# Attention with a mixture of experts on one core: other slots for the routing parts and the row sends

## The reference

```
xn = layernorm(x)
out = x + attention(xn) + experts(xn)

attention: 16 heads of width 8, causal;
  scores = q k^T / sqrt(8) - log1p(decay_h * log1p(distance))
  y = softmax(scores) v,  times w_proj

experts: 8 experts, 128 -> 512 -> 128
  probs = softmax(xn Wr^T); the two best experts of each token,
  their weights normalised to sum 1
  sum over the two of weight * (silu(xn W1_e^T) W2_e^T)
```

## Time and profile before

| | |
|---|---|
| median of three runs | 505.39 us |
| the profiled execution's own time | 506.12 us |
| its span, first to last instruction | 504.40 us |
| granted TensorE clock, mean | 0.997 |
| busy: PE, DVE, ACT, POOL | 478.1, 365.7, 336.6, 366.2 us |
| sends: 64, mean of one | 982 ns |
| POOL's subtractions: 388, mean of one | 493 ns |
| DVE's score instructions: 512, mean of one | 485 ns |

### The profile page before, as it was taken

One profiled execution on the slowest core, in us unless ns is written; L12 is line 12 of the kernel. 1 busy time (PEld: TensorE's weight loads), 2 busy tenths in 40 slices (PEclk: granted clock), 3 DMA queues, 4 the chain that ended last, 5 costly groups with the idle time before them and its releaser, 6 DMA issues.

```text
span 504.4 us, 13425 instructions
## 1 busy us (share of the span) xinstructions
PE 478.1 (95%) x4294; PEld 346.7 (69%) x4294; DVE 365.7 (73%) x1407; ACT 336.6 (67%) x621; POOL 366.2 (73%) x591
## 2 busy tenths in 40 slices
PE   6769899999999999999999999989999999999997
PEld 5645465555664665566566556689999999999564
DVE  7888989988999989989889897733333333333887
ACT  4789878888888888887988888752233233232762
POOL 3587987889888889889889888734454554555784
PEclk9998999999999999999999999999999999999999
DMA  6479790780470461353255153877676777672634
GB/s 188 126 278 286 201 215 16 213 199 18 133 215 28 143 182 57 122 158 102 90 159 138 51 183 112 227 223 238 199 210 208 210 208 207 191 216 69 246 118 140
DMA packets 72755, 82.24 MB, mean 163 GB/s; under 512 B 8638, under 2 KB 52704, under 8 KB 72688
## 3 DMA queue, kind: packets, MB, share of 16 engines
q1 hardware_dynamic: 68368, 72.91, 50.3%
q0 software_dynamic: 4320, 8.47, 4.7%
HBM read 49.94 MB, written 31.86 MB: 162 GB/s over the span
## 4 chain that ended last, share of the span: by engine, by line
PE 69%; DVE 17%; ACT 10%; issue 2%; DMA 1%; SPq 0%; ACTq 0%; DVEq 0%
PE psT L1498 22%; PE psT L1585 13%; PE ps L1558 12%; PE psO L1518 11%; DVE scores L1268 8%; PE ps L1470 6%; ACT probs L1008 4%; ACT scores L965 3%; PE psM L1446 2%; DVE x_all L608 2%; PE ps L1549 1%; ACT values L992 1%; DVE xt L1122 1%; DMA w_qkv<-w_attn 1%; DVE probs L1054 1%
## 5 line engine op out<-in xcount | busy, mean ns | idle before, releaser
L1268 DVE CUSTOM_DVE_ANT_0 scores<-ps,wdist 128x256 f32<-128x256 f32 (+3 forms) x512 | 217.3, 485 | 22.6 <-PE ps L1470 21.8
L1008 ACT ACTIVATE probs<-psT 128x512 f32<-128x512 f32 x320 | 173.8, 597 | 50.3 <-PE psT L1498 49.1
L875 POOL TENSOR_SCALAR scores<-scores,row_max 128x256 f32<-128x256 f32 (+3 forms) x388 | 185.3, 493 | 29.2 <-DVE row_max L1268 28.1
L1498 PE MATMUL psT<-ident,scores 128*128 128x128 f32 x1280 | 176.3, 281 | 5.7 <-ACT probs L1008 5.6
L1498 PEld LDWEIGHTS psT<-ident,scores 128*128 128x128 f32 x1280 | 137.7, 141 | 64.0 <-issue 46.3
L894 POOL DMA_INDIRECT picked_dram<-scores,row_ring x71 | 69.8, 983 | 70.0 <-DVE scores L1349 66.8
L1017 ACT ACTIVATE scores<-ps 128x512 f32<-128x512 f32 x71 | 42.3, 598 | 91.4 <-PE ps L1558 91.4
L1518 PE MATMUL psO<-probs,values 128*32 128x512 f32 (+3 forms) x1024 | 88.4, 441 | 0.0
L965 ACT ACTIVATE scores<-scores,row_max 128x512 f32<-128x512 f32 x124 | 83.0, 727 | 0.0
L1585 PE MATMUL psT<-xn_all,scores 128*128 x568 | 75.4, 276 | 1.6 <-ACT scores L1017 1.6
L1558 PE MATMUL ps<-scores,wdist 128*128 128x128 f32 x568 | 74.9, 275 | 0.6 <-DMA wdist<-w1t 0.6
(11 more groups left out here) (169 smaller groups left out, 295.3 us busy)
## 6 DMA issues: line engine op xcount, KB each, us to landing
wdist<-w1t SPq DMA_DIRECT2D x71, 256.0 KB, 3.4
k_rows<-k_dram SPq DMA_DIRECT2D x64, 96.0 KB, 3.0
q_rows<-q_dram SPq DMA_DIRECT2D x64, 96.0 KB, 2.9
row_ring<-rows_dram SPq DMA_DIRECT2D x71, 65.0 KB, 2.9
rows_dram<-row_ring SPq DMA_DIRECT2D x6, 650.0 KB, 6.3
k_dram<-k_parts SPq DMA_DIRECT2D x7, 384.0 KB, 2.4
q_dram<-q_parts SPq DMA_DIRECT2D x7, 384.0 KB, 2.6
xn_all<-picked_dram SPq DMA_DIRECT2D x4, 512.0 KB, 7.4
```

The lines of the kernel that those rows point to most:

```text
L875: last = nc.gpsimd.tensor_scalar(part, part, -1.0, row_max[:, r, tile, quad:quad + 1], ALU.mult, ALU.add)
L1008: nc.scalar.activation(probs[:, at.ring(2), w, :], psT[:, w % 2], ACT.Exp, scale=-1.0).then_inc(exp_ready, 1)
L1268: last = nc.vector.tensor_tensor_reduce(out=scores[:, r, u, col:col + n], in0=bank[:, col:col + n], in1=wdist[:, at.g * QUADS + quad, SEQ ...
L1498: last = nc.tensor.transpose(psT[:, w % 2, place * P:(place + 1) * P], scores[:, at.ring(2), u, col + key * P:col + (key + 1) * P], ident[:])
```

## The change

Three tables change, and nothing else. The routing parts stand two to a slot in slots 2 to 9, behind score steps 1 and 4 (the second and the last; slot 4 has R6 behind step 2 and CT behind step 4). Sends begin at slot 10 in place of slot 8, four in every slot. The second 32 begin at slot 18 in both; the last ones are now in slot 25, before in slot 27.

```
-ROUTE = {2: {0: ("R1",), 1: ("R2",), 3: ("R3",)},
-         3: {0: ("R4",), 1: ("R5",), 3: ("R6",)},
-         4: {0: ("R7", "GX"), 1: ("CT",), 3: ("R8",)},
-         5: {0: ("R9",), 3: ("R10",)},
-         6: {0: ("R11",), 3: ("R12",)},
-         7: {0: ("R13",), 3: ("R14",)},
-         8: {0: ("R15",)},
-         11: {0: ("R16",)},
-         12: {0: ("R17",)}}
-FIRST_SEND_SLOT = 8
+ROUTE = {2: {1: ("R1",), 4: ("R2",)},
+         3: {1: ("R3",), 4: ("R4",)},
+         4: {1: ("R5",), 2: ("R6",), 4: ("CT",)},
+         5: {1: ("R7",), 4: ("GX",)},
+         6: {1: ("R8",), 4: ("R9",)},
+         7: {1: ("R10",), 4: ("R11",)},
+         8: {1: ("R12",), 4: ("R13",)},
+         9: {1: ("R14",), 4: ("R15",)},
+         11: {1: ("R16",)},
+         12: {1: ("R17",)}}
+FIRST_SEND_SLOT = 10
...
-SENDS = (3, 3, 3, 4, 3, 3, 3, 4, 3, 3)
+SENDS = (4,) * 8
 SECOND_PICK_SLOT = FIRST_SEND_SLOT + len(SENDS)
```

## The result

The change makes the kernel slower: a median of 515.84 us (513.31 to 517.82) against 505.52 us (504.28 to 506.87) for the kernel before, timed beside it. The ratio is 1.0203 with a 95% interval of 1.0175 to 1.0231, thus +8.8 to +11.7 us. The forecast was 513.3 us, 7.9 us above the median of before; measured are 10.3.

What follows compares the result with a forecast made beforehand. PE was taken to bound the kernel, with DVE, ACT and POOL close behind and POOL full once issue gaps count. From 505.39 us, +9.9 for the sends and -2.0 for the routing gave 513.3 us, range 510.3 to 517.3.

Steps and rivals of the forecast that it cites:

- Part 1: Slots 10 to 25: four sends a slot make POOL the bound, its slot 10.56 us, costing +9.9 us.
- (a): Rival for slots 10 to 25: sends stay hidden behind PE, only routing counts, 503.4 us; chance 0.05.
- (b): Rival: two-deep score buffers absorb POOL's backlog, only two new scaling stalls count, 505.8 us; chance 0.04.
- Part 2: DVE's scaling step in slots 12, 16, 20, 24: all stall above 2 us, adding only 0.54 us each while POOL bounds.
- with four sends ahead all four should look like this: Scaling steps of slots 12, 16, 20 and 24 should all resemble the two earlier ones of 2.97 us.
- Part 3: Slots 2 to 9: moving routing parts behind DVE's score steps removes waits of PE, -2.0 us, bounds -4.1 to +1.0.
- what is late next: Routing parts newly ahead of score steps in slots 4, 6, 9 and 10 cause new lateness, charged 0.6 us.
- the prediction's last paragraph: Signs of right or wrong; among them, in slots 3 to 9 PE's waits for DVE fall from 3.5 to near 1 us.
- the counts: PE's 31 small products behind slot 4's fifth score step, waiting for R6 on DVE: 0 taken, 1.07 us at most.
- Rival (d): Routing in slots 2 to 9 gains nothing, its waits only move: 515.3 us, chance counted inside the forecast's 0.86.
- Part 4: Last sends end two slots earlier, so SyncE's expert loads start earlier: 0 taken, -0.6 us at most.
- rival (c): DVE becomes a bound too: output scaling in odd slots waits beside POOL, 0.5 us in eight slots, 517.3 us; chance 0.05.

Runs made afterwards that it cites:

- e1: Old routing table with the new sends, four a slot from slot 10, against the kernel before: 517.54 us, ratio 1.0251.
- e3: The changed kernel with its sends at five a slot (the last slot two) from slot 10: 526.84 us, ratio 1.0441 to the kernel before.
- e4: The changed kernel with only the second 32 sends spread by the old threes and fours from slot 18: 509.09 us, ratio 1.0097 to before.
- e7: The changed kernel with three routing parts moved, R5 to slot 3, R6 and R8 within their slots: 516.99 us, ratio 1.0250 to before.
- e5: The kernel before with its four-send slots moved from 11, 15, 21 and 25 to 8, 12, 18 and 22: 504.76 us, ratio 0.9995.
- e8: The kernel before with its four-send slots moved to 8, 12, 20 and 24: 503.63 us, ratio 0.9971.
- e2: The changed kernel with the old sends from slot 8 and R12 to R15 all in slot 8: 505.91 us, ratio 1.0007 to before.
- e6: The kernel before with four-send slots 8, 12, 18 and 22 and a rearranged routing ending its R9 to R15 in slot 8: 505.60 us, ratio 1.0027.

## Why the prediction was right, step by step

**Part 1, the sends: right, and 1.7 us too small.** POOL became the bound, by the count of its issue gaps that the busy share leaves out. e1 has the loss with the sends alone, e3 has double of it for one more send, and in e4 it stops with the fours: that leaves no room for rivals (a), hidden sends, and (b), a backlog that buffers take up. Forecast from 10 to 26 were 309.8 - 139.59 = 170.2 us, measured 171.96. Three places make up the difference. The first four sends with their gaps took 143.20 - 137.37 = 5.83 us, and the prediction had taken 4.99 for them from a later slot: +0.84, from the two long sends in the lines above (1.25 and 1.51 us). The fifteen slots from 143.20 to 304.29 took 161.09 us against 15 x 10.56 + 4 x 0.54 = 160.56: +0.53, of which the twelve of an odd slot, 5.66 us beside 5.50 in slot 22, are the larger part; the outputs are scaled there. Last, the granted clock of TensorE fell in this execution to 0.50, its level of 1.2 GHz, behind a wait of PE for POOL at the first turn of group 25. A row of PE's timeline and a window of the stretch:

```profile
286.78 1.87 PE L1499 MATMUL psT<-ident,scores 128*128 128x128 f32 x8 [1.57 <-POOL scores L876]
...
287.00:290.30 3.30, 3.30 (x12) 1.80 (x10) 0.82 (x6) 1.19 (x2) 2.83 (x6) 0.50 0.00 0
```

The eight turns took 1.87 us for 1.09, POOL then waited its 0.23 us for DVE in slot 25, and at group 26 PE was no longer held by POOL: its turn comes at 308.45, 0.49 us behind the eighth subtraction (304.29 + 8/12 x 5.51 = 307.96), and 0.1 had been taken: about +0.4. In e7, whose code from slot 10 on is the same, the clock stayed at 1.00 there, POOL has no such wait, and 10 to 26 takes 308.83 - 137.39 = 171.44 us. By this comparison some 0.5 of the 1.7 us belong to this execution's clock and not to the sends.

PE's waits were to be 2 to 3 us for POOL in four slots; they are 7.1 us in sixteen, 1.8 in four, and the rest of its idle time stands before score steps, 2.6 us in ten short waits for DVE, and at the scaling step.

**Part 2, the scaling step: the price held, its reading failed.** All four were to be above 2 us. The timeline of DVE, slots 12 and 20, and of POOL at those moments:

```profile
155.47 4.10 DVE L1123 TENSOR_TENSOR xt<-xt,yt 128x512 f32<-128x512 f32 x1
...
240.93 0.96 DVE L1123 TENSOR_TENSOR xt<-xt,yt 128x512 f32<-128x512 f32 x1
```

```profile
155.36 1.28 POOL L876 TENSOR_SCALAR scores<-scores,row_max 128x128 f32<-128x128 f32 x3
...
240.59 1.45 POOL L876 TENSOR_SCALAR scores<-scores,row_max 128x384 f32<-128x384 f32 x2
```

The step of slot 12 took longer than any in the kernel before, 4.10 us; slots 16, 20 and 24 took 0.95, 0.96 and 0.94. The step that failed is "with four sends ahead all four should look like this": a slot of four is not the cause, but a lag of POOL that lets DVE arrive in a certain place of the twelve. By slot 16 the lag had grown, DVE arrived earlier among them (1.25 us behind the start of the twelve, for 1.59 in slot 12), and the stall was gone. In the ten profiles there are 70 scaling steps. Of those that began while POOL had a subtraction of 128x384 running, 48, none took over 1.23 us (0.69 at least). Nine began in one of 128x256: 2.43 to 2.97 us. Eight began in one of 128x128: four of these with no subtraction behind it took 0.82, four with more of them behind it 4.03 to 4.11. The other five, with POOL idle or at a 128x512 one, took 0.68 to 2.23. e5 moved the fours only, which moved the stalls; e8 put three slots of threes between a four and the next scaling step, which removed them. Why the step gets through in the first case after one subtraction or two, and in the others after four to eight, no run here shows; no run changed the subtractions' sizes.

The rule of the Trainium skill that the prediction weighed ("SBUF — State Buffer", SBUF: two separate sides: the pair belongs to whoever starts first, for that one instruction) fits the 48 short ones. It doesn't fit 13 of 70, from 2.43 to 4.11 us, during which four to eight of POOL's subtractions ended, nor two of e3 that began with POOL idle and took 1.49 and 2.23; for these the measurement decides.

For the sum it made no difference, as the prediction said: twelve subtractions with a scaling step took 5.92 to 6.02 us beside 5.50, its 0.54 nearly, and the one long stall cost PE 1.0 us in slot 12, where POOL was late anyway.

**Part 3, the routing: -2.0 forecast, -0.8 in the stretch, of which -0.5 is the routing's** (e1 to after); alone (e2) it gave nothing. The other 0.3 to 0.4 came with the later start of the sends (e1 against before). Gone are all four waits of the earlier trace rows, 2.8 us, where the forecast had 2.5 of them going. The step that failed is "what is late next", charged 0.6. PE's waits from 40 to 132 us in after, and their places:

```profile
PE psT L1499 <- ACT probs L1009: 1.6, 3, 1.1
PE ps L1471 <- DVE row_max L1269: 1.1, 2, 1.0
PE psM L1426 <- DVE picks L1179: 0.6, 1, 0.6
```

```profile
58.06 1.11 PE L1499 MATMUL psT<-ident,scores 128*128 128x128 f32 x8 [1.13 <-ACT probs L1009]
...
69.80 0.27 PE L1426 MATMUL psM<-picks,before 128*128 128x256 bf16 x1 [0.57 <-DVE picks L1179]
...
92.49 0.39 PE L1471 MATMUL ps<-k_rows,q_rows 48*128 48x384 bf16 x4 [0.98 <-DVE row_max L1269]
```

DVE's waits did fall from 3.5 to 1.1 us, as the prediction's last paragraph had it. But ACT's single wait of 0.6 became three of 1.6, the longest, 1.13, in slot 3, where ACT had worked without a pause since 51.78 us; the counts waited 0.57 us for R6, where 0 had been taken and 1.07 allowed; and in slot 6 DVE has R8 (1.1 us), a transpose of outputs (0.71) and a subtraction for the next batch (0.67) in a row between the second and the third score step, and PE's last one waits 0.98. Rival (d), that the waits only move, was nearer than the sum. The window of groups 1 to 9 suggests why: DVE is busy 87.79 of 93.88 us, 94%, and PE itself 96%, so little was to be won. A wait that is removed there comes back elsewhere: e6 and e7 each took named waits away and got others, 95.82 and 94.20 us against 94.72 and 93.88.

**Part 4, the end of the sends: right.** SyncE's wait of 8.7 us went, and the expert loop kept its time within its spread.

**The time.** 515.84 us lies in the range of 510.3 to 517.3. With what was measured in place of the terms, +11.6 for the sends and -0.8 for the routing, the sum is +10.8; +10.3 is measured. Both terms missed to the same side, by 1.7 and 1.2 us, so nothing cancelled. That the range reached far enough above the forecast is owed to rival (c), DVE as a second bound, which set its high end. Its mechanism showed, at a smaller price. The scaling of outputs in odd slots did wait beside POOL's subtractions:

```profile
L1309 DVE TENSOR_TENSOR y_q<-o_q,rden x15: 424/491/566, 66.8 to 487.2; 128x256 f32<-128x256 f32 x15
...
L1310 DVE TENSOR_TENSOR y_q<-o_q,rden x15: 424/479/1982, 63.3 to 494.5; 128x256 f32<-128x256 f32 x15
```

(ns min/median/max, before and after.) In six of the odd slots from 11 to 23 it took 1.50 to 1.98 us, and these steps together took 7.2 us more than before, most of the 8.8 that DVE is busy longer. But DVE took that from its idle time: no subtraction of POOL waited for DVE in slots 11 to 24, and what shows on the path is the 0.16 us by which the twelve of an odd slot are longer.

## What to carry to other kernels

Count an engine's issue gaps as work: POOL was 87 to 89% busy in the stretch before the change, and had no time for one send more in a slot. Compare what each engine has to do in one period with the period of the engine that sets the pace, four slots against four slots; where it fits only on average, put the larger portions where the lag has time to run off ahead of the next step that collides with it. And where an engine is 94% busy over a stretch, moving its instructions mostly moved the waits; whether fewer instructions would remove them no run here tried.

## What the runs showed of the hardware that wasn't expected

A send that began early in the two-operand step that DVE runs for R16 took 0.55 us longer: it began 0.06 us behind that step in after and took 1.51 us, where its neighbours took 0.96. The step itself:

```profile
139.05 0.74 DVE L1243 TENSOR_TENSOR row_ring<-row_ring,ends_a 128x568 f32<-128x568 f32 x1
```

So it is in e3, e4 and e7, which have R16 in the same place (1.50 to 1.52 us). In e1, where R16 came behind score step 0, the first send had begun 0.10 us ahead of the step and took 1.25 us, as first sends do without it, and the second took its usual time:

```profile
141.62 0.96 POOL L887 DMA_INDIRECT rows_dram<-xn_all  x1 [0.30 <-issue]
```

The Trainium skill's page "SBUF — State Buffer" (Who interferes with whom) infers that a tensor_tensor on DVE doesn't stall the making of descriptors, as the two need different sides of the pair; these four sends speak against it, and that the one that began first kept its time agrees with the page's rule of who holds the pair. Sends that began in the last 0.12 us of an output scaling, ten in before, kept the 1.01 to 1.02 us that the first send of a slot takes.

The very first send of an execution takes 1.25 us in all ten profiles, in whichever slot it stands.

The granted clock of TensorE between 35 and 47 us differs between executions of code that is nearly the same there: 1.00 in after, 0.86 in before, 0.72 in e1, means over stretches at 2.4 and at 1.2 GHz; from the turn of group 0 to that of group 1 they took 12.18, 12.79 and 13.88 us. PE had been busy 6.9 of the ten microseconds ahead of it in after and e1 alike. That is 1.7 us between two profiles that no edit made, and a reason to compare stretches rather than spans. It also fell where PE waited for POOL: between 132 and 312 us once in after and e4, twice in e1, three times in e3, and not in before or e7. e7 has the same wait of PE for POOL, 1.58 us, at the place where it fell in after.
